# Linear attention with every query normalized, then three more blocks: norms by quarters of tokens, and an earlier start of factors and projections

## The chip, the cores and the metric

The kernel runs on one core of a Trainium2 chip. A core has a matrix engine (TensorE, here PE, with its weight loads as PEld), a vector engine (VectorE, DVE), an activation engine (ScalarE, ACT), a general engine (GpSimd, POOL) and queues that move data (issued by SyncE, SP). Each engine takes its instructions in order, and they wait for one another by semaphores. Matrix results land in eight banks of PSUM, each 128 rows by 512 floats. The metric is the device time of one execution in microseconds (us), lower being better.

## The reference

Four blocks follow one another, each added to its input and normalized over the 256 features: a linear attention, a selected low-rank update, a softmax attention and a mixture of experts. The change touches only the first:

```
q = hidden_states @ Wq.T + bq            # 4 x 512 tokens x 256 -> 16 heads of 128
k, v = ...                               # 4 key heads of 128, each used by 4 query heads
sq, sk = elu(q) + 1, elu(k) + 1
kv = einsum('bhsd,bhse->bhde', sk, v)
norm = einsum('bhsd,bhd->bhs', sq, sk.sum(axis=2))
attn = einsum('bhsd,bhde->bhse', sq, kv) / (norm[..., None] + 1e-6)
x = layernorm(x + attn.reshape(b, s, H * D) @ Wo.T)
```

## The kernel before

`layer0_attention` computes this block, phase 1, one batch of 512 tokens after another; the four batches run the same code. Everything is kept with features on the 128 partitions and the 512 tokens along the row. A product that needs more than one pass of the reduced float type is made from high and low parts of both operands, three matmuls for one (`split_passes`).

For a batch PE does, in this order:

- keys and values for four tiles of 128 tokens (`key_value`), then the sums over tokens (`state`);
- sixteen queries (`query`), one head each, six matmuls of 512 columns into one of three banks `bank_q`. ScalarE makes two passes over it (`query_exp`, lines 426 and 428), VectorE the third (line 522), which gives `sq` and frees the bank;
- between them the eight output maps (`output_map`, line 331): a head pair's kv times Wo, in `bank_a`. ScalarE and VectorE split each into high and low parts (`map_hi`, `map_lo`), of which four pairs are kept;
- four norms (`norm`, line 316), one for every four queries: the sum of sq times the keys' sum for each token. The weights `ksel` are 128x32, so four heads' matmuls stand on four column groups of the array. Norms 0 and 1 make the first half of `bank_n`'s use, norms 2 and 3 the second;
- after norms 1 and 3, VectorE adds a small number and inverts (`invert`, `invert_tokens`), ScalarE and VectorE split the result (`factor_hi`, `parts`) into `rn_parts`;
- sixteen factors (`factor`, line 345): one matmul spreads a head's inverted norm over all partitions, again into one of the three `bank_q`. VectorE multiplies `sq` by it (line 601, signal `scaled`), ScalarE takes the high part `s_hi` (line 468), and the low part `s_lo` is made by VectorE for even n (line 533) and by GpSimd for odd n (line 229);
- sixteen projections (`project`, line 361), twelve matmuls of 256 columns each, from `s_hi`, `s_lo` and a map's parts, all summed in `bank_y`.

The order on each engine is written out by hand. In the last stage PE takes factor n+2, then projection n, with a map behind n = 1, 3, 5 and 7. VectorE scales query n, and for odd n it then makes the low part of n-1:

```python
for n in range(H0):
    dve.wait_ge(bc_done, H0 * b + n + 1)
    dve.tensor_tensor(sq[:, n, :], sq[:, n, :], bank_q[(H0 + n) % 3][:, :], ALU.mult).then_inc(scaled, 1)
    if n % 2 == 1:
        scaled_lo(b, n - 1)
```

`s_hi` and `s_lo` have two buffers, so ScalarE makes the high part of n only when projection n-2 is done. In the texts below, query, factor and projection are counted from 0 to 15, norm from 0 to 3, map from 0 to 7.

Of the kernel before, what the change touches and what calls it, by code (L numbers as in the profile page):

```python
# [10 lines left out]
F32 = mybir.dt.float32  # L11
F32R = mybir.dt.float32r
# [4 lines left out]
P = 128  # L17
# [9 lines left out]
ORDER0 = [(g, j) for j in range(J0) for g in range(G0)]  # L27

# [85 lines left out]
def layer0_attention(nc, a, kept):  # L114

    with ExitStack() as ctx:
# [18 lines left out]
        pick_raw, pick = sb("pick_raw", [H0]), sb("pick", [H0], F32R)  # L135
# [7 lines left out]
        ksel = sb("ksel", [G0, J0, 32])  # L143
# [3 lines left out]
        den, rn = sb("den", [T]), sb("rn", [T])  # L147
        rn_c, rn_parts = sb("rn_c", [T], F32R), sb("rn_parts", [2, T], F32R)
        m_hi, m_lo = sb("m_hi", [4, 2 * D], F32R), sb("m_lo", [4, 2 * D], F32R)
        s_hi, s_lo = sb("s_hi", [2, T], F32R), sb("s_lo", [2, T], F32R)  # L150
# [31 lines left out]
        PARTS_AT = 10  # L182
        MAP_AT = (4, 6, 14, 15)
# [10 lines left out]
        def _(sp):  # L194
# [12 lines left out]
            with sp.Fori(0, B - 1) as b:  # L207
                after = sp.snap(b + 1)
                sp.wait_ge(xT_hi_ready, after)
                sp.wait_ge(xT_lo_ready, after)  # L210
                sp.dma_start(xT[:, :, :], a["xT"][:, bass.ds(after, 1)].rearrange("p o k n -> p (o k) n")).then_inc(xT_in, 16)
# [9 lines left out]
        def _(pool):  # L221
# [3 lines left out]
            def scaled_lo(b, n):  # L225
# [3 lines left out]
                pool.tensor_tensor(s_lo[:, 1, :], sq[:, n, :], s_hi[:, 1, :].bitcast(F32), ALU.subtract).then_inc(s_lo_ready[1], 1)  # L229
# [31 lines left out]
        def _(pe):  # L261
# [30 lines left out]

            def query(b, n):
                g, j = ORDER0[n]
                hd = slice((J0 * g + j) * DH0, (J0 * g + j + 1) * DH0)
                if n < 3:
                    at_least(pe, scaled, H0 * b)
                else:
                    pe.wait_ge(sq_ready, H0 * b + n - 2)
                i = 0  # L300
                for k in range(KD):
                    for lhs, rhs in split_passes(wq_hi[:, k, hd], wq_lo[:, k, hd], xT_hi[:, k, :], xT_lo[:, k, :]):
                        mm = pe.matmul(bank_q[n % 3][:, :], lhs, rhs, start=i == 0, stop=i == 3 * KD - 1)  # L303
# [3 lines left out]
            def norm(b, j):  # L307
# [27 lines left out]
            def factor(b, n):  # L335
# [5 lines left out]
                if n < 3:  # L341
                    pe.wait_ge(sq_ready, H0 * b + H0 + n - 2)
                else:
                    pe.wait_ge(scaled, H0 * b + n - 2)
                pe.matmul(bank_q[(H0 + n) % 3][:, :], pick[:, h:h + 1].broadcast_to([P, P]), rn_parts[:, n // (H0 // 2), :],  # L345
                          start=True, stop=True).then_inc(bc_done, 1)

            def project(b, n):
# [8 lines left out]
                for t in range(NT):  # L357
                    tok = slice(t * P, (t + 1) * P)
                    for i, (lhs, rhs) in enumerate(split_passes(s_hi[:, n % 2, tok], s_lo[:, n % 2, tok], m_hi[:, m, cols], m_lo[:, m, cols])):
# [9 lines left out]
            def body(b, first):  # L369
                pe.wait_ge(xT_hi_ready, b + 1)  # L370
                pe.wait_ge(xT_lo_ready, b + 1)
# [11 lines left out]
                for n in range(3, H0):  # L383
# [3 lines left out]
                    if n % G0 == 1 and n > G0:  # L387
                        norm(b, n // G0 - 1)
# [16 lines left out]
        def _(act):  # L405
            def split_x(b):
                act.wait_ge(xT_in, 16 * (b + 1))
                at_least(act, q_done, H0 * b)
                act.activation(xT_hi[:, :, :], xT[:, :, :], ACT.Copy).then_inc(xT_hi_ready, 1)
# [6 lines left out]
            def factor_hi(b, half_):  # L416
                act.wait_ge(rn_ready, 2 * (2 * b + half_ + 1))
# [3 lines left out]
            def query_exp(b, n):  # L421
# [4 lines left out]
                act.activation(eq[:, n % 3, :], bank_q[n % 3][:, :], ACT.Relu, bias=bq_neg[:, h:h + 1], scale=-1.0).then_inc(eq_capped, 1)  # L426
# [1428 lines left out]
```

## Time and profile before

| | us |
|---|---|
| Runs, median of 3 (lowest to highest) | 835.08 (834.54 to 848.41) |
| The profiled execution | 842.74 |
| its span, first to last instruction | 840.7 |
| PE busy, weight loads beside it | 723.7, 486.0 |
| DVE busy | 528.6 |
| ACT busy | 410.0 |
| POOL busy | 106.4 |

The profile comes from one execution. Busy time is the time in which an engine had an instruction under way. Matmuls are pipelined: one begins before the one ahead has ended, so a matmul's own length is more than the pace at which they follow one another, and the pace is read from the starts. A line of the timeline gives the start, the length, the engine, the line of the code, what is written from what, and in brackets the idle time ahead and who ended it.

### The profile page before, as it was taken

To read this page: it belongs to the slowest core of one execution; us is meant where nothing else is said; L and a number is where in the kernel's file an instruction comes from. 1 tells how busy PE (TensorE), PEld (TensorE's weight loads), DVE (VectorE), ACT (ScalarE), POOL (GpSimd) and SP (SyncE) were. 2 spreads that over 40 slices of the span, in tenths; PEclk is the share of its full clock that TensorE was granted. 3 is DMA by queue.
4 is the path that set the end of the run, shared out by engine and by line. 5 is a ranking of instruction groups with operands and counts; after the bars stand their busy time and mean duration, and the time that the engine had idled before them with its cause. 6 is when DMAs were issued, how large, how long until landed. Compare 5 with 4: busy or idle time off the path is not lost.

```text
span 840.7 us, 10896 instructions
## 1 busy us (share of the span) xinstructions
PE 723.7 (86%) x3836; PEld 486.0 (58%) x3836; DVE 528.6 (63%) x1135; ACT 410.0 (49%) x742; POOL 106.4 (13%) x102
## 2 busy tenths in 40 slices
PE   4798999889989998934678998899999999999764
PEld 3667886778768776833433453355555545455454
DVE  3568556855586558553365777777978787762243
ACT  3474347434754465421202674576556665556422
POOL 0301320132013301315000100010002000000000
PEclk9999999999999999975755896899999999879968
DMA  9200000010000100010650182028100840000000
GB/s 350 76 1 0 27 0 1 1 40 0 0 0 0 69 0 0 0 47 1 75 75 2 23 102 29 2 38 95 23 2 17 93 70 2 1 2 27 26 0 26
DMA packets 13588, 28.22 MB, mean 34 GB/s; under 512 B 2593, under 2 KB 3433, under 8 KB 13033
## 3 DMA queue, kind: packets, MB, share of 16 engines
q1 hardware_dynamic: 13544, 27.67, 17.6%
q8 instruction: 24, 0.39, 0.2%
q14 instruction: 20, 0.16, 0.1%
HBM read 12.59 MB, written 2.10 MB: 17 GB/s over the span
## 4 chain that ended last, share of the span: by engine, by line
PE 39%; DVE 10%; ACT 3%; issue 2%; DMA 2%; POOL 1%; SPq 0%; ACTq 0%; POOLq 0%; DVEq 0%
PE bank_st L1012 8%; PE bank_c L1025 6%; DVE nmax L1512 5%; PE side L962 4%; PE side L1083 3%; PE bank_s L993 3%; PE side L1114 2%; PE side L1043 2%; PE side L945 1%; DMA ks<-qk_lo 1%; PE side L914 1%; PE side L976 1%; ACT xk L1249 1%; DVE ln_bn L1470 1%; PE bank_t L1033 1%
## 5 line engine op out<-in xcount | busy, mean ns | idle before, releaser
L1512 DVE TENSOR_REDUCE nmax<-bank_s 128x1 f32<-128x512 f32 x256 | 164.8, 685 | 75.6 <-PE bank_s L993 74.8
L1293 ACT ACTIVATE shared<-bank_st 128x512 f32<-128x512 f32 x256 | 139.1, 596 | 78.2 <-PE bank_st L1012 77.4
L993 PE MATMUL bank_s<-ks,qs 48*128 48x512 f32 x256 | 117.6, 526 | 19.4 <-DVE nmax L1512 11.6
L1012 PE MATMUL bank_st<-qs,ks 50*128 50x512 f32 x256 | 106.2, 487 | 8.3 <-ACT shared L1293 4.7
L361 PE MATMUL bank_y<-m_hi,s_lo 128*128 128x256 f32 x256 | 75.4, 294 | 16.4 <-ACT s_hi L468 8.4
L522 DVE SCALAR_TENSOR_TENSOR sq<-bank_q,bq,eq 128x512 f32<-128x512 f32 x64 | 46.6, 738 | 51.3 <-ACT eq L428 51.3
L468 ACT ACTIVATE s_hi<-sq 128x512 fp32r<-128x512 f32 x64 | 40.4, 631 | 78.8 <-PE bank_y L361 66.1
L1025 PE MATMUL bank_c<-shared,v 128*32 128x512 f32 x512 | 76.9, 676 | 0.9 <-ACT shared L1293 0.9
L1012 PEld LDWEIGHTS bank_st<-qs,ks 50*128 50x128 f32 x256 | 43.2, 201 | 57.3 <-issue 32.1
L361 PE MATMUL bank_y<-m_lo,s_hi 128*128 128x256 f32 x256 | 73.9, 288 | 0.0
L361 PE MATMUL bank_y<-m_hi,s_hi 128*128 128x256 f32 x256 | 73.7, 288 | 0.0
L229 POOL TENSOR_TENSOR s_lo<-sq,s_hi 128x512 fp32r<-128x512 f32 x32 | 43.4, 1355 | 225.2 <-ACT s_hi L468 225.2
L993 PEld LDWEIGHTS bank_s<-ks,qs 48*128 48x128 f32 x256 | 47.5, 209 | 38.9 <-DVE nmax L1512 29.7
L601 DVE TENSOR_TENSOR sq<-sq,bank_q 128x512 f32<-128x512 f32 x64 | 43.4, 679 | 32.5 <-PE bank_q L345 32.5
L361 PEld LDWEIGHTS bank_y<-m_hi,s_lo 128*128 128x128 f32 x256 | 50.3, 197 | 21.8 <-issue 13.0
L426 ACT ACTIVATE eq<-bank_q,bq_neg 128x512 f32<-128x512 f32 x64 | 44.1, 689 | 35.1 <-PE bank_q L303 33.4
L303 PE MATMUL bank_q<-xT_hi,wq_lo 128*128 128x512 f32 x128 | 54.7, 427 | 0.0
L361 PEld LDWEIGHTS bank_y<-m_lo,s_hi 128*128 128x128 f32 x256 | 50.4, 197 | 1.7
L303 PE MATMUL bank_q<-xT_lo,wq_hi 128*128 128x512 f32 x128 | 50.6, 396 | 0.0
L303 PE MATMUL bank_q<-xT_hi,wq_hi 128*128 128x512 f32 x128 | 50.6, 395 | 0.0
L846 POOL TENSOR_TENSOR ln_rstd<-ln_var,half 128x4 f32<-128x4 f32 x12 | 12.1, 1012 | 303.7 <-DVE ln_var L111 303.7
L361 PEld LDWEIGHTS bank_y<-m_hi,s_hi 128*128 128x128 f32 x256 | 50.4, 197 | 0.0
(242 smaller groups left out, 1353.2 us busy)
## 6 DMA issues: line engine op xcount, KB each, us to landing
qs<-qk_hi SPq DMA_DIRECT2D x16, 256.0 KB, 5.5
ks<-qk_hi SPq DMA_DIRECT2D x16, 256.0 KB, 10.0
xT<-in_xT SPq DMA_DIRECT2D x4, 512.0 KB, 5.1
sq<-in_wqT SPq DMA_DIRECT2D x2, 1024.0 KB, 9.0
wo<-in_woT SPq DMA_DIRECT2D x1, 2048.0 KB, 12.6
xs<-in_x SPq DMA_DIRECT2D x1, 2048.0 KB, 17.5
qs<-qk_lo SPq DMA_DIRECT2D x8, 256.0 KB, 7.8
ks<-qk_lo SPq DMA_DIRECT2D x8, 256.0 KB, 10.5
```

The source lines that it names most:

```text
L229: pool.tensor_tensor(s_lo[:, 1, :], sq[:, n, :], s_hi[:, 1, :].bitcast(F32), ALU.subtract).then_inc(s_lo_ready[1], 1)
L303: mm = pe.matmul(bank_q[n % 3][:, :], lhs, rhs, start=i == 0, stop=i == 3 * KD - 1)
L361: mm = pe.matmul(bank_y4[:, t, :], lhs, rhs, start=n == 0 and i == 0 and t % 2 == 0, stop=n == H0 - 1 and i == 2, skip_group_check=True)
L426: act.activation(eq[:, n % 3, :], bank_q[n % 3][:, :], ACT.Relu, bias=bq_neg[:, h:h + 1], scale=-1.0).then_inc(eq_capped, 1)
L468: act.activation(s_hi[:, n % 2, :], sq[:, n, :], ACT.Copy).then_inc(s_hi_ready, 1)
L522: dve.scalar_tensor_tensor(out=sq[:, n, :], in0=bank_q[n % 3][:, :], scalar=bq1[:, h:h + 1], in1=eq[:, n % 3, :], op0=ALU.add, op1=ALU.max ...
L601: dve.tensor_tensor(sq[:, n, :], sq[:, n, :], bank_q[(H0 + n) % 3][:, :], ALU.mult).then_inc(scaled, 1)
L993: pe.matmul(bank_s[u % 2][:, :], qs[part, b % 2, slot, t * P:(t + 1) * P], ks[part, b % 2, slot, :], start=True, stop=True).then_inc(s_don ...
L1012: pe.matmul(bank_st[u % 2][:, :], ks[part, b % 2, slot, kt * P:(kt + 1) * P], qs[part, b % 2, slot, :], start=True, stop=True).then_inc(st ...
L1025: mm = pe.matmul(bank_c[32 * j:32 * j + 32, :], v[:, b % 2, kt, 4 * g + j, :], probs[:, (4 * s + j) % SLOTS, :], start=kt == 0, stop=kt == 3)
L1293: act.activation(probs[:, u % SLOTS, :], bank_st[u % 2][:, :], ACT.Exp, scale=SCALE1).then_inc(p_ready, 1)
L1512: dve.tensor_reduce(nmax[:, g, t, j:j + 1], bank_s[u % 2][:, :], AX.X, ALU.max, negate=True).then_inc(max_ready, 1)
```

## The change

The norms are taken by quarters. A norm's four matmuls of 512 columns become sixteen of 128 columns, whose weights put each quarter of the tokens in rows of its own, so that the inverted norms of all 512 tokens fill 128 columns. The additions, inversions and splits on VectorE and ScalarE shrink from 512 columns to 128. A factor's one matmul of 512 columns becomes four of 128, each with another column of `pick` as weights.

The order is rewritten. Factors 0, 1 and 2 and projections 0 and 1 stand between queries 12 and 15, and the three banks are taken in turn by queries and factors together (`USES`). From projection 3 on, PE takes factor n+1 and then projection n. The maps are made after queries 4, 6, 8 and 10 and projections 3, 5, 7 and 9. `s_hi` and `s_lo` get three buffers. The splits of x and the statistics are cut in parts.

```diff
+USES = ([("query", n) for n in range(13)] + [("factor", 0), ("query", 13), ("factor", 1), ("query", 14), ("factor", 2), ("query", 15)]
+        + [("factor", n) for n in range(3, H0)])
...
-        s_hi, s_lo = sb("s_hi", [2, T], F32R), sb("s_lo", [2, T], F32R)
+        s_hi, s_lo = sb("s_hi", [3, T], F32R), sb("s_lo", [3, T], F32R)
...
-                for g in range(G0):
-                    mm = pe.matmul(bank_n[32 * g:32 * g + 32, :], ksel[:, g, j, :], sq[:, G0 * j + g, :],
-                                   start=j % 2 == 0, stop=j % 2 == 1)
+                for q in range(QUARTERS):
+                    tok = slice(q * P, (q + 1) * P)
+                    for g in range(G0):
+                        mm = pe.matmul(bank_n[32 * g:32 * g + 32, (j // 2) * P:(j // 2 + 1) * P], ksel[:, g, QUARTERS * (j % 2) + q, :],
+                                       sq[:, G0 * j + g, tok], start=j % 2 == 0 and q == 0, stop=j % 2 == 1 and q == QUARTERS - 1)
...
-                pe.matmul(bank_q[(H0 + n) % 3][:, :], pick[:, h:h + 1].broadcast_to([P, P]), rn_parts[:, n // (H0 // 2), :],
-                          start=True, stop=True).then_inc(bc_done, 1)
+                q_bank_free(b, "factor", n)
+                for q in range(QUARTERS):
+                    mm = pe.matmul(q_bank("factor", n)[:, q * P:(q + 1) * P], pick[:, QUARTERS * h + q:QUARTERS * h + q + 1].broadcast_to([P, P]),
+                                   rn_parts[:, n // (H0 // 2), :], start=True, stop=True)
+                mm.then_inc(bc_done, 1)
...
                 pe.wait_ge(setup_done, 4)
                 factor(b, 0)
+                query(b, 13)
+                norm(b, 2)
                 factor(b, 1)
-                norm(b, J0 - 1)
-                for n in range(H0):
-                    if n + 2 < H0:
-                        factor(b, n + 2)
+                query(b, 14)
+                project(b, 0)
+                factor(b, 2)
+                query(b, 15)
+                project(b, 1)
+                factor(b, 3)
+                project(b, 2)
+                norm(b, 3)
+                for n in range(3, H0):
+                    if n + 1 < H0:
+                        factor(b, n + 1)
                     project(b, n)
-                    if n % 2 == 1 and n < 8:
-                        output_map(b, 4 + n // 2)
+                    if n in (3, 5, 7, 9):
+                        output_map(b, 4 + (n - 3) // 2)
...
-                    act.wait_ge(scaled, H0 * b + n + 1)
-                    at_least(act, y_done, H0 * b + max(0, n - 1))
-                    act.activation(s_hi[:, n % 2, :], sq[:, n, :], ACT.Copy).then_inc(s_hi_ready, 1)
+            def scaled_hi(b, n):
+                act.wait_ge(scaled, H0 * b + n + 1)
+                at_least(act, y_done, H0 * b + max(0, n - 2))
+                act.activation(s_hi[:, n % 3, :], sq[:, n, :], ACT.Copy).then_inc(s_hi_ready, 1)
...
+                scale(b, 0)
+                query(b, 12)
+                scaled_lo(b, 0)
+                scale(b, 1)
+                query(b, 13)
+                query(b, 14)
+                scale(b, 2)
+                scaled_lo(b, 2)
+                query(b, 15)
+                scale(b, 3)
+                scale(b, 4)
+                invert(b, 1)
+                scaled_lo(b, 4)
+                for n in range(5, H0):
+                    scale(b, n)
+                    if n % 2 == 1 and n > 5:
                         scaled_lo(b, n - 1)
```

What stands in PE's row, first batch, at the turn from queries to projections. L303 is a query, L345 a factor, L316 a norm, L361 a projection. Before, from the end of query 15:

```order
L303 MATMUL bank_q<-xT_hi,wq_hi 128x512
L331 MATMUL bank_a<-wo,kvT 128x256 [waits m_lo_ready]
L331 MATMUL bank_a<-wo,kvT 128x256
L345 MATMUL bank_q<-rn_parts,pick 128x512 [waits sq_ready,parts_ready,setup_done]
L345 MATMUL bank_q<-rn_parts,pick 128x512 [waits sq_ready]
L316 MATMUL bank_n<-sq,ksel 32x512 [waits sq_ready]
L316 MATMUL bank_n<-sq,ksel 32x512 x3
L345 MATMUL bank_q<-rn_parts,pick 128x512 [waits sq_ready]
L361 MATMUL bank_y<-m_hi,s_lo 128x256 [waits m_lo_ready,s_lo_ready_even,s_hi_ready]
```

After the change, from factor 1 on; L361 is now the factor, L319 a query, L334 the norm and L378 the projection:

```order
L361 MATMUL bank_q<-rn_parts,pick 128x128 [waits sq_ready]
L361 MATMUL bank_q<-rn_parts,pick 128x128 x3
L319 MATMUL bank_q<-xT_hi,wq_lo 128x512 [waits scaled]
...
L378 MATMUL bank_y<-m_hi,s_lo 128x256 [waits m_lo_ready,s_lo_ready_even,s_hi_ready]
...
L361 MATMUL bank_q<-rn_parts,pick 128x128 [waits sq_ready]
L361 MATMUL bank_q<-rn_parts,pick 128x128 x3
L319 MATMUL bank_q<-xT_hi,wq_lo 128x512 [waits scaled]
...
L378 MATMUL bank_y<-m_hi,s_lo 128x256 [waits s_lo_ready_odd,s_hi_ready]
```

Before, three factors and the last norm stood between the last query and the first projection. After it, projection 0 follows query 14 and projection 1 follows query 15, and each has one factor fewer ahead of it.

VectorE's row in the last stage, after the change, from the scaling of query 7. L571 scales, L565 makes the low part of an even query, L559 that of a map, L518 that of x:

```order
L571 TENSOR_TENSOR sq<-sq,bank_q 128x512 [waits sq_ready,bc_done]
L565 TENSOR_TENSOR s_lo<-sq,s_hi 128x512 [waits scaled,s_hi_ready]
L571 TENSOR_TENSOR sq<-sq,bank_q 128x512 [waits sq_ready,bc_done]
L559 TENSOR_TENSOR m_lo<-bank_a,m_hi 128x512 [waits m_hi_ready]
L571 TENSOR_TENSOR sq<-sq,bank_q 128x512 [waits sq_ready,bc_done]
L565 TENSOR_TENSOR s_lo<-sq,s_hi 128x512 [waits scaled,s_hi_ready]
L518 TENSOR_TENSOR xT_lo<-xT,xT_hi 128x512 [waits q_done,xT_hi_ready]
```

These are the scaling of 7, the low part of 6, the scaling of 8, a map, the scaling of 9, the low part of 8: as before the change, the low part of an even query stands behind the scaling of the next query. What moved is PE's side, where the factor of that next query has one projection less of lead.

## Rows read from the trace of the kernel before

**Rows 1.** Windows: us, busy time and count by engine, granted clock, DMA share, GB/s
```profile
51.80:104.40 52.60, 47.81 (x299) 39.85 (x298) 36.62 (x48) 26.47 (x42) 10.32 (x8) 0.97 0.03 11
136.16:190.67 54.51, 48.05 (x299) 39.87 (x298) 37.93 (x57) 26.46 (x42) 11.36 (x8) 0.97 0.06 16
222.41:276.45 54.04, 47.84 (x299) 39.72 (x298) 37.93 (x57) 26.46 (x42) 11.37 (x8) 0.97 0.00 0
308.20:360.50 52.30, 46.64 (x299) 38.43 (x297) 36.35 (x56) 25.41 (x41) 10.31 (x8) 1.00 0.00 0
360.50:840.70 480.20, 403.71 (x2014) 223.90 (x2012) 307.97 (x794) 229.38 (x463) 39.00 (x50) 0.84 0.25 34
```

**Rows 2.** Timeline of PE, second batch, a norm and an output map among queries
```profile
137.33 0.39 PE L303 MATMUL bank_q<-xT_hi,wq_hi 128*128 128x512 f32 x1
...
138.99 0.39 PE L303 MATMUL bank_q<-xT_lo,wq_hi 128*128 128x512 f32 x1
...
147.54 0.39 PE L303 MATMUL bank_q<-xT_lo,wq_hi 128*128 128x512 f32 x1
147.77 0.39 PE L303 MATMUL bank_q<-xT_hi,wq_hi 128*128 128x512 f32 x1
...
149.10 0.40 PE L303 MATMUL bank_q<-xT_lo,wq_hi 128*128 128x512 f32 x1
```

**Rows 3.** Timeline of PE, the same batch, factors two projections and a map apart
```profile
161.28 0.58 PE L345 MATMUL bank_q<-rn_parts,pick 128*128 128x512 f32 x1
...
165.47 0.58 PE L345 MATMUL bank_q<-rn_parts,pick 128*128 128x512 f32 x1
```

**Rows 4.** Waits of PE from 30 to 361: us in total, times, longest
```profile
PE bank_n L316 <- DVE sq L522: 6.7, 8, 1.1
```

**Rows 5.** Timeline of PE, second batch: first projection, and the batch's end
```profile
155.93 0.36 PE L361 MATMUL bank_y<-m_hi,s_lo 128*128 128x256 f32 x1 [1.78 <-ACT s_hi L468]
...
180.88 0.36 PE L361 MATMUL bank_y<-m_hi,s_lo 128*128 128x256 f32 x1 [1.46 <-POOL s_lo L229]
...
182.38 0.40 PE L345 MATMUL bank_q<-rn_parts,pick 128*128 128x512 f32 x1
...
189.16 0.36 PE L361 MATMUL bank_y<-m_hi,s_lo 128*128 128x256 f32 x1 [0.87 <-POOL s_lo L229]
```

**Rows 6.** Windows: a stretch just behind the turn of the second batch
```profile
156.30:159.60 3.30, 3.30 (x17) 3.20 (x17) 3.30 (x4) 0.63 (x1) 0.79 (x1) 0.51 0.02 5
```

**Rows 7.** Groups by form, second to fourth batch: busy, mean ns of one
```profile
L522 DVE SCALAR_TENSOR_TENSOR sq<-bank_q,bq,eq 128x512 f32<-128x512 f32 x48 | 34.9, 738 | 33.8 <-ACT eq L428 33.8
...
L544 DVE RECIPROCAL rn<-den 128x256 f32<-128x256 f32 x12 | 20.9, 1746 | 0.1
...
L426 ACT ACTIVATE eq<-bank_q,bq_neg 128x512 f32<-128x512 f32 x48 | 33.1, 689 | 20.7 <-PE bank_q L303 19.4
```

**Rows 8.** Timeline of PE and of its loads (PEld), same batch
```profile
123.95 0.95 PE L290 MATMUL bank_a<-ones,sk_sum 128*128 128x1 f32 x8
...
152.65 0.16 PEld L316 LDWEIGHTS bank_n<-sq,ksel 128*32 128x32 f32 x8 [1.12 <-DVE sq L522]
...
180.85 0.19 PEld L361 LDWEIGHTS bank_y<-m_hi,s_lo 128*128 128x128 f32 x1 [1.75 <-ACT s_hi L468]
180.96 0.19 PEld L361 LDWEIGHTS bank_y<-m_lo,s_hi 128*128 128x128 f32 x1
```

**Rows 9.** Timelines of DVE, ACT and POOL, the end of the same batch
```profile
182.81 0.69 DVE L601 TENSOR_TENSOR sq<-sq,bank_q 128x512 f32<-128x512 f32 x1 [1.53 <-PE bank_q L345]
184.46 0.69 DVE L601 TENSOR_TENSOR sq<-sq,bank_q 128x512 f32<-128x512 f32 x1 [0.96 <-PE bank_q L345]
185.07 0.68 DVE L533 TENSOR_TENSOR s_lo<-sq,s_hi 128x512 fp32r<-128x512 f32 x1
...
186.95 0.63 ACT L468 ACTIVATE s_hi<-sq 128x512 fp32r<-128x512 f32 x1 [2.03 <-PE bank_y L361]
...
187.74 1.28 POOL L229 TENSOR_TENSOR s_lo<-sq,s_hi 128x512 fp32r<-128x512 f32 x1 [2.69 <-ACT s_hi L468]
```

More of the change, by code:

```diff
@@ L291, in state, with q_bank_free @@
                 mm.then_inc(ksum_done, 1)
+            def q_bank_free(b, kind, n):
+                k = USE[kind, n]
+                if k < 3:
+                    at_least(pe, scaled, H0 * b)
+                elif USES[k - 3][0] == "query":
+                    pe.wait_ge(sq_ready, H0 * b + USES[k - 3][1] + 1)
+                else:
+                    pe.wait_ge(scaled, H0 * b + USES[k - 3][1] + 1)
             def query(b, n):
@@ L295, in query @@
                 hd = slice((J0 * g + j) * DH0, (J0 * g + j + 1) * DH0)
[L296 to L299, printed above, removed]
+                q_bank_free(b, "query", n)
                 i = 0
@@ L302, in query @@
                     for lhs, rhs in split_passes(wq_hi[:, k, hd], wq_lo[:, k, hd], xT_hi[:, k, :], xT_lo[:, k, :]):
-                        mm = pe.matmul(bank_q[n % 3][:, :], lhs, rhs, start=i == 0, stop=i == 3 * KD - 1)
+                        mm = pe.matmul(q_bank("query", n)[:, :], lhs, rhs, start=i == 0, stop=i == 3 * KD - 1)
                         i += 1
@@ L382, in body @@
                 pe.wait_ge(wo_in, 16)
-                for n in range(3, H0):
+                for n in range(3, 13):
                     query(b, n)
@@ L521, in query @@
                 dve.wait_ge(eq_ready, H0 * b + n + 1)
-                dve.scalar_tensor_tensor(out=sq[:, n, :], in0=bank_q[n % 3][:, :], scalar=bq1[:, h:h + 1], in1=eq[:, n % 3, :],
+                dve.scalar_tensor_tensor(out=sq[:, n, :], in0=q_bank("query", n)[:, :], scalar=bq1[:, h:h + 1], in1=eq[:, n % 3, :],
                                          op0=ALU.add, op1=ALU.max).then_inc(sq_ready, 1)
@@ L584, in body @@
                     for r in range(2):
-                        cp = dve.tensor_copy(dst[:, 4 * r:4 * r + 3 * 33 + 1:33], bank_a[1][:, g:g + 1].broadcast_to([P, J0]))
+                        cp = dve.tensor_copy(dst[:, 16 * r:16 * r + 7 * 33 + 1:33], bank_a[1][:, g:g + 1].broadcast_to([P, 2 * QUARTERS]))
                 cp.then_inc(ksel_ready, 1)
-                for n in range(3, H0):
+                for n in range(3, 12):
                     query(b, n)
+                    if n in (3, 5) and last:
+                        residual_stats(b - 1, (0, 1) if n == 3 else (2, 3))
                     if n == 7 and last:
-                        residual_stats(b - 1)
-                    if n == PARTS_AT:
+                        residual_merge(b - 1)
+                    if n == 9:
                         invert(b, 0)
-                    if n in (PARTS_AT, PARTS_AT + 1):
-                        invert_tokens(b, 0, n - PARTS_AT)
-                    if n == PARTS_AT + 4:
+                    if n == 10:
                         parts(b, 0)
@@ L622, in _ @@
             residual(B - 1)
-            residual_stats(B - 1)
+            residual_stats(B - 1, range(NT))
+            residual_merge(B - 1)
 def by_tile(x):
@@ L1795, in constants @@
         for j in range(J0):
-            pick[32 * g + j, J0 * g + j] = pick[32 * g + 4 + j, J0 * g + j] = 1.0
-            part_c[32 * g + j], part_c[32 * g + 4 + j], part_m[32 * g + 4 + j] = 1.0, -1.0, 1.0
+            for q in range(QUARTERS):
+                row, col = 32 * g + QUARTERS * (j % 2) + q, QUARTERS * (J0 * g + j) + q
+                pick[row, col] = pick[row + 16, col] = 1.0
+                part_c[row], part_c[row + 16], part_m[row + 16] = 1.0, -1.0, 1.0
     return {"pick": pick, "part_c": part_c, "part_m": part_m, "ones": np.ones((P, 1), np.float32),
```

108 lines of the change are left out of this document (54 added, 54 removed).

## The prediction

> **What bounds the kernel now.** I first cut the span into stretches [rows 1]. The attention phase takes 360.5 us and the rest 480.2 us; the diff touches only the first. The first four rows are the piece of each batch that the change rebuilds, from query 9 (the tenth) to the end of projection 15: 52.60, 54.51, 54.04 and 52.30 us, mean 53.36. In each of them PE is busy for some 48 us and no other engine for more than 38, so PE is what there is to shorten, by taking away work or waits.
>
> The PE timeline of the second batch gives the prices of its work. A query matmul follows the one before after 0.23 us, so a query (six) is 1.40 [rows 2]. A norm: from 137.33 to 138.99 is 1.66 us, less two of these paces, 1.19. An output map: 147.77 to 149.10 is 1.33, less the same, 0.86 [rows 2]. Between the factors at 161.28 and 165.47 lie two projections, two factors and a map: 4.19 us without a gap [rows 3]. A factor is one 512-column matmul of the query's pace, 0.235, so a projection is (4.19 - 0.86 - 0.47)/2 = 1.43. The sum from query 9 on: 7 queries 9.8, 3 norms 3.6, 16 factors 3.8, 16 projections 22.9, 6 maps 5.2, together 45.2 us. What is left, 53.36 - 45.2 = 8.2 us a batch, is waiting and slow clock, and that is all a new order can win.
>
> Where it sits: PE waits for the last query of norm 2 and again for that of norm 3, 6.7 us in eight waits, 0.84 each [rows 4]. For the first scaled query it waits 1.78, and near the end for GpSimd's low part, 1.46 and 0.87 us [rows 5]. After the gaps of the turn from queries to projections the granted clock is 0.51 for 3.3 us, the 1.2 GHz level [rows 6]; that costs about 1.6. It happens in three of the four batches.
>
> **The change part by part.** *The turn.* Factors 0 to 3 and projections 0 to 2 move between the queries. They give PE work where it waited for norm 3 and for the first scaled query. I replayed the new order by hand with the prices above (and those of factor and norm below), from query 9 at 0: norm 1 at 1.40, query 10 at 2.74, the map 4.14, query 11 at 5.00, query 12 at 6.40, factor 0 from 7.80 to 8.24. Query 13 takes the bank of query 11, since a factor now has a turn in the three banks, so it waits until VectorE has finished query 11. That is some 0.2 for the last matmul's way out (0.39 long at a pace of 0.23 [rows 2]), 0.69 on ScalarE [rows 7] and again 0.63, as its pass for a high part [rows 9], 0.74 on VectorE [rows 7] and some 0.07 between: 8.73, and 8.78 with a guess of 0.05 until PE starts, a wait of 0.55. From there norm 2 runs at 10.2, factor 1 at 11.5, query 14 at 12.0, projection 0 at 13.4, factor 2, query 15 to 16.6, projection 1, factor 3, projection 2 to 19.9. ScalarE has query 15 late, at 18.3, VectorE at 19.1, still ahead of norm 3. Projection 3 begins at 21.8. So of the waits and the slow clock of the turn, some 5 us with 1.6 of clock, nearly all is won.
>
> *Smaller factors on VectorE.* The reciprocals go from four of 128x256, 1.75 us each [rows 7], to two of 128x128 a batch, at half the elements for half the price, so 5.2 us of VectorE. It was not the bound; worth nothing but the earlier factors, which are in the replay. Halved splits of x, split statistics and the third buffer are hidden likewise: the third buffer takes away the waits of the batch's end, since a high part no longer waits for the projection just before. Without this cover they cost 1.46 and 0.87 again.
>
> *A factor in four matmuls.* Each quarter has its own weights (another column of pick), so each needs a 128x128 load. The trace has no matmul of 128 columns in the reduced float type. From below: columns alone, a quarter of 0.235 each, so 0 more per factor. From above: eight one-column matmuls with 128x128 loads take 0.95 us, 0.12 each [rows 8]. After a gap the next load starts 0.11 after the first [rows 8], and a queued load has nothing else to wait for there. I take 0.11 a quarter, 0.44 a factor, nearer the upper row: +0.2 x 16 = +3.3 us a batch. The Trainium skill, "TensorE: Matmul & The Clock Gate", LDWEIGHTS, says the load takes its columns over 1.2 GHz, 107 ns; the spacing agrees. The same page, Back-to-back issue gap, gives about 81 ns a matmul for a stream of loads and 128-column matmuls; by that a factor would be 0.32 and the batch 1.9 us shorter than I say.
>
> *A norm in sixteen matmuls.* The columns are as many as before, in rounds of four on four column groups. From below nothing more; from above each of eight rounds shows its load, about 0.11, so +0.85. The eight loads of a norm all pass in 0.16 us from its start, while its first matmuls stream [rows 8]: the second set is loaded behind the first. So I stay low: +0.15 a norm, 0.6 a batch. The same page, Part 3, says that a load overlaps matmuls in flight only when their row groups differ; here they are the same. That speaks against this change and is rival C.
>
> *The lead of the factors.* This is the term I rest on. Before, PE issued factor n+2 ahead of projection n; now factor n+1. VectorE still makes the low part of an even query n only after it has scaled query n+1. So an even projection waits for a chain that starts with the factor just ahead of it. Its price: factor to scaling 0.43 (182.38 to 182.81) [rows 5, 9], of which 0.235 is the factor's own; in quarters the last starts at 0.33 and its columns and way out take 0.25, so 0.58. Then scaling holds VectorE 0.60, and the low part takes 0.68 [rows 9]; 0.05 until PE starts, the guess above. Sum 1.91 us from the factor's start, while PE has 0.44 to do: it waits 1.47. That is so for n = 6, 8, 10, 12, 14: 7.35 a batch. Nothing is queued that could fill it, as PE goes in order; factor n+2, behind it, is late by as much, so the wait comes back at each even projection. An odd projection's chain: 0.58, scaling 0.69, ScalarE 0.63, GpSimd 1.28, with 0.04, 0.16 and 0.14 between [rows 9], 3.5 us from its factor. For n = 7 to 13 PE reaches it at 1.91 + 1.43 + 0.44 = 3.8, no wait. For n = 5, whose even neighbour has no such wait, 1.1; 0.2 each at n = 3 and 15.
>
> **The sum.** Waits after: 0.55 + 0.2 + 1.1 + 7.35 + 0.2 = 9.4. Work: 45.2 + 3.3 + 0.6 = 49.1. A batch has 58.5 us against 53.36, +5.1; four of them +20. The profiled execution was 842.74 us (span 840.7) and would be 863; the median is 835.08, 7.7 lower, and the same step on it gives 855. The spread of the runs shown, 834.54 to 848.41, is likely the clock of the later phase (0.84 granted [rows 1]), which I hold equal.
>
> **The rivals.** A, as above: 855. Its own range is 849 to 862: a norm's extra between 0 and 0.3 instead of 0.15 is 2.4 either way, and the later phase may move by a few us.
> B, a quarter costs its columns only (0.06): a batch is 16 x 0.2 = 3.2 us shorter, four 12 to 13: 843. For it: loads run beside matmuls in all of [rows 3]; against: the 0.11 spacing of [rows 8].
> C, the small tiles' loads show: 0.7 us more in each of 16 norms, +11: 866. Against it the eight loads in 0.16 us.
> D, the waits pull the clock down again: three gaps in a row of 1.47 us. Each stretch like [rows 6] costs 1.6; with two or three a batch, +16: 871. Against it: gaps of 1.46 to 0.87 us a few us apart at the end of a batch [rows 5] went with no fall.
> E, no waits at the even projections, the other side. The place is the head of projections 6 to 14. If the third buffer and one factor of lead were enough, the 7.35 us go: 855 - 29 = 826. It decides where such a wait is under (7.35 - 5.1)/5 = 0.45 us instead of 1.47; at 0.45 the time is that of before. For it: in [rows 3] the chain never shows. Against: there the factor led by two projections, and the order rows put scaling n+1 ahead of low part n.
>
> **How the numbers follow.** Chances: A 0.50, B 0.17, C 0.10, D 0.09, E 0.14. The likeliest is A, 855. The range of 838 to 868 leaves out E and most of D, and holds B and C. A measurement here can tell about 2% from no change: below 818.4 or above 851.8. Slower: C, D and 0.38 out of A, 0.57. Within: B, 0.10 out of E and 0.12 out of A, 0.39. Faster: what is left of E, helped by the later phase's clock, 0.04.
>
> **What would show it.** PE gaps of about 1.5 us ahead of projections 6, 8, 10, 12 and 14, released by VectorE's low part; none at 7 to 13 odd; a pair of projections every 6.1 us with a map, 5.2 without, where it is 4.19 now. Loads of the quarters 0.11 apart. A norm of 1.2 to 1.4 us. Granted clock 1.00 from query 9 to the end of each batch. The span after the attention phase within a few us of 480. I am wrong if the even gaps are under 0.5 us (E), if the quarters are 0.06 apart (B), or if the later phase moves by more than 10 us.

## The result, and the profile after

| | before | after |
|---|---|---|
| Runs beside each other, median (lowest to highest) | 840.54 (834.54 to 848.41), 4 | 863.66 (859.31 to 868.02), 4 |
| The profiled execution | 842.74 | 859.31 |
| its span | 840.7 | 857.5 |

The change makes the kernel slower: the ratio of the times is 1.03, with a 95% interval of 1.0168 to 1.0431. The four runs of after lie in two pairs, near 859.5 and 867.8; the profile is of one of the lower pair.

The windows of after, cut as [rows 1] cut before. The columns are us, busy time and count of PE, PEld, DVE, ACT and POOL, granted clock, DMA share, GB/s:

```profile
52.64:110.61 57.97, 49.34 (x416) 44.70 (x415) 29.19 (x47) 24.52 (x42) 10.92 (x8) 1.00 0.03 10
143.25:201.45 58.20, 49.48 (x416) 44.74 (x415) 29.69 (x52) 24.52 (x42) 10.79 (x8) 1.00 0.06 15
234.09:292.27 58.18, 49.47 (x415) 44.70 (x414) 29.69 (x52) 24.52 (x42) 10.80 (x8) 1.00 0.00 0
324.91:383.00 58.09, 49.38 (x415) 44.63 (x413) 28.54 (x50) 23.49 (x40) 10.31 (x8) 1.00 0.00 0
383.00:857.50 474.50, 396.64 (x2014) 220.62 (x2013) 308.67 (x794) 228.89 (x463) 38.91 (x50) 0.85 0.25 34
```

The attention phase ends at 383.0 instead of 360.5, +22.5 us. The phase behind it, whose code is the same, took 474.5 instead of 480.2, 5.7 less at a clock of 0.85 instead of 0.84. Together that is the +16.8 of the two spans. From query 9 to projection 15 a batch takes 58.11 in the mean. In after the third map stands ahead of query 9 (behind query 8), so the same work as in [rows 1] is that plus a map of 0.86: 58.97 against 53.36, +5.6 a batch, +22.4 in four. The clock is 1.00 in each of the four; before it was 0.97 in three of them.

PE's waits in the attention phase (us in total, times, longest):

```profile
PE bank_y L378 <- ACT s_hi L459: 20.0, 14, 1.4
PE bank_y L378 <- DVE s_lo L565: 8.3, 6, 1.4
...
PE bank_y L378 <- POOL s_lo L238: 4.3, 4, 1.1
PE bank_q L319 <- DVE sq L554: 1.8, 4, 0.4
```

L378 is the projection, L319 a query. Of before, the waits for norms of [rows 4], 6.7 us, are gone, and so are those for the first scaled query. In their place stand twenty waits of 1.4 us, 28.3 us in two rows, five in each batch.

One of them, the timeline of PE in the first batch around projection 8 (start, length, engine, line, operation, and in brackets the idle time ahead and who is held to have ended it):

```profile
84.40 0.36 PE L378 MATMUL bank_y<-m_hi,s_lo 128*128 128x256 f32 x1 [1.43 <-ACT s_hi L459]
...
88.47 0.74 PE L361 MATMUL bank_q<-rn_parts,pick 128*128 128x128 f32 x4
90.64 0.35 PE L378 MATMUL bank_y<-m_hi,s_lo 128*128 128x256 f32 x1 [1.43 <-ACT s_hi L459]
...
92.14 0.56 PE L361 MATMUL bank_q<-rn_parts,pick 128*128 128x128 f32 x4
92.54 0.33 PE L378 MATMUL bank_y<-m_hi,s_lo 128*128 128x256 f32 x1
92.71 0.28 PE L378 MATMUL bank_y<-m_lo,s_hi 128*128 128x256 f32 x1
...
96.88 0.35 PE L378 MATMUL bank_y<-m_hi,s_lo 128*128 128x256 f32 x1 [1.43 <-ACT s_hi L459]
...
102.25 0.36 PE L378 MATMUL bank_y<-m_hi,s_lo 128*128 128x256 f32 x1 [1.43 <-ACT s_hi L459]
```

and what the other engines do in it, over the gap from 89.2 to 90.64:

```profile
89.25 0.69 DVE L571 TENSOR_TENSOR sq<-sq,bank_q 128x512 f32<-128x512 f32 x1 [1.46 <-PE bank_q L361]
89.85 0.69 DVE L565 TENSOR_TENSOR s_lo<-sq,s_hi 128x512 fp32r<-128x512 f32 x1
89.97 0.63 ACT L459 ACTIVATE s_hi<-sq 128x512 fp32r<-128x512 f32 x1 [1.60 <-DVE sq L571]
```

At 88.47 PE issues factor 9. VectorE sat idle until it came (1.46), scales query 9 at 89.25, and only then makes the low part of query 8, from 89.85 to 90.54. PE starts projection 8 at 90.64. The row names ScalarE, but that instruction is the high part of query 9, which projection 8 does not use and which ended at 90.60 by chance; the other six of the twenty waits do name VectorE's low part. At 92.54 projection 9 follows its factor without a wait.

### The profile page after: what moved, and what is told of

It reads as the page before. It is cut to its first block, busy times and chain, and to the rows that moved or that the text cites. A ratio compares the mean times of both kernels' runs of the same rounds, so it can differ in the third digit from the quotient of the medians.

```text
span 857.5 us, 12122 instructions
## 1 busy us (share of the span) xinstructions
PE 727.3 (85%) x4412; PEld 508.7 (59%) x4412; DVE 504.4 (59%) x1131; ACT 405.2 (47%) x746; POOL 106.1 (12%) x102
## 4 chain that ended last, share of the span: by engine, by line
PE 36%; DVE 10%; ACT 3%; issue 2%; DMA 2%; POOL 1%; SPq 0%; ACTq 0%; POOLq 0%; DVEq 0%
PE bank_st L1059 8%; PE bank_c L1072 6%; DVE nmax L1559 5%; PE side L1130 3%; PE side L1009 3%; PE bank_s L1040 2%; PE side L1161 2%; DMA ks<-qk_lo 1%; PE side L992 1%; PE side L1090 1%; PE side L961 1%; ACT xk L1296 1%; DVE ln_bn L1517 1%; PE side L1023 1%; PE bank_t L1114 1%
## 5 line engine op out<-in xcount | busy, mean ns | idle before, releaser
L1059 PE MATMUL bank_st<-qs,ks 50*128 50x512 f32 x256 | 104.3, 479 | 9.2 <-ACT shared L1340 5.7
L378 PE MATMUL bank_y<-m_hi,s_lo 128*128 128x256 f32 x256 | 76.1, 297 | 33.0 <-ACT s_hi L459 20.0
L571 DVE TENSOR_TENSOR sq<-sq,bank_q 128x512 f32<-128x512 f32 x64 | 43.9, 686 | 81.5 <-PE bank_q L361 81.5
L1072 PE MATMUL bank_c<-shared,v 128*32 128x512 f32 x512 | 73.8, 650 | 0.9 <-ACT shared L1340 0.9
L378 PE MATMUL bank_y<-m_lo,s_hi 128*128 128x256 f32 x256 | 72.2, 282 | 0.0
L378 PE MATMUL bank_y<-m_hi,s_hi 128*128 128x256 f32 x256 | 72.1, 282 | 0.0
L378 PEld LDWEIGHTS bank_y<-m_hi,s_lo 128*128 128x128 f32 x256 | 48.6, 190 | 37.0 <-ACT s_hi L459 21.6
L452 ACT ACTIVATE eq<-bank_q,bq_neg 128x512 f32<-128x512 f32 x64 | 43.9, 686 | 35.7 <-PE bank_q L319 33.8
L319 PE MATMUL bank_q<-xT_hi,wq_lo 128*128 128x512 f32 x128 | 54.9, 429 | 1.8 <-DVE sq L554 1.8
L319 PE MATMUL bank_q<-xT_lo,wq_hi 128*128 128x512 f32 x128 | 50.5, 395 | 0.0
L319 PE MATMUL bank_q<-xT_hi,wq_hi 128*128 128x512 f32 x128 | 50.5, 394 | 0.0
L378 PEld LDWEIGHTS bank_y<-m_lo,s_hi 128*128 128x128 f32 x256 | 48.8, 191 | 0.4
L378 PEld LDWEIGHTS bank_y<-m_hi,s_hi 128*128 128x128 f32 x256 | 48.7, 190 | 0.0
```

The lines of the kernel that those rows point to most:

```text
L319: mm = pe.matmul(q_bank("query", n)[:, :], lhs, rhs, start=i == 0, stop=i == 3 * KD - 1)
L378: mm = pe.matmul(bank_y4[:, t, :], lhs, rhs, start=n == 0 and i == 0 and t % 2 == 0, stop=n == H0 - 1 and i == 2, skip_group_check=True)
L452: act.activation(eq[:, n % 3, :], q_bank("query", n)[:, :], ACT.Relu, bias=bq_neg[:, h:h + 1], scale=-1.0).then_inc(eq_capped, 1)
L571: dve.tensor_tensor(sq[:, n, :], sq[:, n, :], q_bank("factor", n)[:, :], ALU.mult).then_inc(scaled, 1)
L1059: pe.matmul(bank_st[u % 2][:, :], ks[part, b % 2, slot, kt * P:(kt + 1) * P], qs[part, b % 2, slot, :], start=True, stop=True).then_inc(st ...
L1072: mm = pe.matmul(bank_c[32 * j:32 * j + 32, :], v[:, b % 2, kt, 4 * g + j, :], probs[:, (4 * s + j) % SLOTS, :], start=kt == 0, stop=kt == 3)
```

## Experiments

All compute the whole result. The end of the attention phase is the start of its last residual addition: 360.74 in before, 383.27 in after. "Period" is the time from one batch's first key matmul to the next one's: 86.26 and 85.78 in before, 90.84 and 90.82 in after.

**1. The lead of the factors, alone.** After with one factor more of lead from projection 3 on, nothing else:

```diff
                 norm(b, 3)
+                factor(b, 4)
                 for n in range(3, H0):
-                    if n + 1 < H0:
-                        factor(b, n + 1)
+                    if n + 2 < H0:
+                        factor(b, n + 2)
                     project(b, n)
```

> The changed kernel with one edit: in the last stage PE issues factor n+2 ahead of projection n, as before the change (factor 4 stands ahead of the loop). Theory of the lead: a factor now starts 2.3 us or more ahead of the even projection that waits for its chain of 1.9 us, so the five waits of 1.43 us a batch and the 1.1 us at projection 5 go. A pair of projections with a map comes every 4.6 us instead of 6.24. The period of a batch falls from 90.8 us by 8, the time by some 32, to 828 to 833, below the kernel before. Rival, the array or ScalarE is the bound anyway (the profile names ScalarE's high part as the releaser of most of these waits): the waits stay at 1 us or more, the time stays above 850.

Measured: 829.25 (828.49 to 830.49), before beside it 842.7, ratio 0.9868 (0.9793 to 0.9944). The attention phase ends at 347.59. The same view of waits as above:

```profile
PE bank_q L319 <- DVE sq L555: 1.8, 4, 0.4
...
PE bank_y L378 <- POOL s_lo L238: 0.9, 4, 0.3
```

All twenty waits are gone. The pair of projections with a map, from factor to factor on PE's timeline:

```profile
168.38 0.74 PE L361 MATMUL bank_q<-rn_parts,pick 128*128 128x128 f32 x4
168.96 0.33 PE L378 MATMUL bank_y<-m_hi,s_lo 128*128 128x256 f32 x1
...
173.00 0.74 PE L361 MATMUL bank_q<-rn_parts,pick 128*128 128x128 f32 x4
```

4.62 us, where after has 6.24 (84.40 to 90.64). The edit issues each factor one projection earlier and gives back 34.4 us of the median and 35.7 of the attention phase; so the missing lead is the cause, and the rest of the change is worth a gain. A batch's period falls by 9.1 (90.84 to 81.75).

**2. The same waits, from VectorE's side.** After with the low part of an even query put ahead of the scaling of the next one:

```diff
                 for n in range(5, H0):
                     scale(b, n)
-                    if n % 2 == 1 and n > 5:
-                        scaled_lo(b, n - 1)
...
+                    if n % 2 == 0:
+                        scaled_lo(b, n)
```

> The changed kernel with one edit: PE keeps its lead of one, but VectorE makes the low part of an even query right after its own scaling and its map, ahead of the scaling of the next query. Theory of the lead: even projections no longer wait for the next factor; now each projection waits for its own factor's chain, 2.7 us for even and 3.5 for odd against 2.3 of PE work ahead. Waits of about 0.4 at even and near 1 at odd projections, a pair with a map every 5.8 us instead of 6.24, 5.0 instead of 5.37 without. Some 8 us less, 850 to 855. Rival, that the order on VectorE has no part in it: the waits stay at the even projections with 1.4 us each, and the time stays at 860.

Measured: 853.62 (852.04 to 860.1), ratio 1.0183 (1.0094 to 1.0271). This is within the expected range and 10.0 less than after. PE's timeline, second batch, every wait from 176.5 on:

```profile
180.82 0.36 PE L378 MATMUL bank_y<-m_hi,s_lo 128*128 128x256 f32 x1 [1.09 <-POOL s_lo L238]
186.72 0.36 PE L378 MATMUL bank_y<-m_hi,s_lo 128*128 128x256 f32 x1 [1.09 <-POOL s_lo L238]
192.09 0.36 PE L378 MATMUL bank_y<-m_hi,s_lo 128*128 128x256 f32 x1 [1.42 <-ACT s_hi L459]
197.11 0.36 PE L378 MATMUL bank_y<-m_hi,s_lo 128*128 128x256 f32 x1 [1.47 <-POOL s_lo L238]
```

The even projections no longer wait at all, not even the 0.4 us that I had expected. But now the odd ones wait for GpSimd's low part, whose chain is longer: 1.09 in the pairs with a map, which come every 5.90 (180.82 to 186.72) instead of 6.24, and 1.42 and 1.47 in those without (the first of them is put down to ScalarE again). So the order on VectorE decides which projection waits. It also decides a part of what is lost, 10.0 us of the 34.4 that the lead gives back; but with one factor of lead there is a wait in every pair.

**3. The quarters, alone.** Norms and factors in quarters, in the order, the lead and the two buffers of before:

```diff
+USES = [("query", n) for n in range(H0)] + [("factor", n) for n in range(H0)]
...
                 factor(b, 1)
...
+                norm(b, J0 - 1)
+                for n in range(H0):
+                    if n + 2 < H0:
+                        factor(b, n + 2)
+                    project(b, n)
+                    if n % 2 == 1 and n < 8:
+                        output_map(b, 4 + n // 2)
```

> The kernel before with the quarters alone: norms in sixteen matmuls, factors in four, inversions of 128 columns; the order on every engine, the lead of two and the two buffers are those of before. Load-bound quarters (0.10 to 0.11 us each): +0.2 us for each of 64 factors, +13, less up to 1 us a batch for VectorE's shorter inversions at the turn: 9 to 13 us more than before. Rival, a quarter costs its columns only: no more than before, or 2 us less.

Measured: 848.13 (845.64 to 853.13), ratio 1.0073 (1.0036 to 1.0111), 5.4 us over before, less than expected. The profiled execution was the longest of the eleven, 853.13, and its attention phase ends at 368.75, 8.0 later than before's. The waits:

```profile
PE bank_y L377 <- ACT s_hi L449: 8.5, 4, 2.2
...
PE bank_y L377 <- POOL s_lo L237: 3.1, 4, 0.9
PE bank_n L333 <- DVE sq L543: 2.1, 4, 0.5
```

Before has 8.4, 7.6 and 6.7 in the rows that answer. What I had left out is that longer factors also fill gaps: the factors' extra work is 16 x 0.2 x 4 = 13, and in these rows the waits fell by 9.0, from 22.7 to 13.7. The sum, some 4, is in line with the median; the profiled execution has some 4 more. These are in the granted clock. The first projection now waits 2.15 where it waited 1.78 [rows 5], and behind it the clock falls, as in [rows 6]. Its timeline and its window:

```profile
157.88 0.55 PE L377 MATMUL bank_y<-m_hi,s_lo 128*128 128x256 f32 x1 [2.15 <-ACT s_hi L449]
```

```profile
157.80:162.00 4.20, 4.12 (x19) 4.16 (x20) 0.85 (x2) 0.63 (x1) 1.25 (x1) 0.50 0.00 0
```

It falls in all four batches, and for longer in two of them. The windows of the second and the fourth batch:

```profile
136.00:194.60 58.60, 54.80 (x431) 49.63 (x430) 33.78 (x58) 27.85 (x46) 10.32 (x8) 0.94 0.06 15
309.00:368.75 59.75, 55.98 (x436) 50.69 (x434) 31.73 (x57) 27.76 (x45) 10.31 (x8) 0.94 0.00 0
```

The first and the third have 0.97, and [rows 1] has 0.97 three times and 1.00 once. The missing share of each window, times its length, is an estimate of what the slow clock cost: some 10.5 us here and 4.8 in before, 5 to 6 more, which covers those 4.

**4. The order, alone.** The order, lead and three buffers of after, with whole norms and factors; only what whole tiles need is moved (inversions in two pieces, the split one query later):

```diff
-                for q in range(QUARTERS):
-                    mm = pe.matmul(q_bank("factor", n)[:, q * P:(q + 1) * P], pick[:, QUARTERS * h + q:QUARTERS * h + q + 1].broadcast_to([P, P]),
-                                   rn_parts[:, n // (H0 // 2), :], start=True, stop=True)
+                mm = pe.matmul(q_bank("factor", n)[:, :], pick[:, h:h + 1].broadcast_to([P, P]), rn_parts[:, n // (H0 // 2), :],
+                               start=True, stop=True)
...
                     if n == 9:
                         invert(b, 0)
+                        invert_tokens(b, 0, 0)
                     if n == 10:
+                        invert_tokens(b, 0, 1)
+                    if n == 11:
                         parts(b, 0)
...
                 invert(b, 1)
                 scaled_lo(b, 4)
+                invert_tokens(b, 1, 0)
```

> The new order alone: norms, factors and inversions whole as before the change, order, lead of one and three buffers as after it (the two halves of an inversion and the split stand one query later where they must). Theory of the lead: the waits at even projections stay, 1.5 us each; a pair with a map comes every 5.85 us instead of 6.24, since a factor is 0.2 shorter and the chain 0.15; the first factor waits up to 2 us for the longer inversion. In sum 3 to 9 us less than the changed kernel, and 10 to 16 more than before. Rival, the quarters are what makes the change slow: about the time of before or less.

Measured: 865.93 (864.46 to 866.91), ratio 1.0307 (1.0229 to 1.0386). The pair is as expected, 5.85 (PE's timeline, second batch, projections 6 and 8):

```profile
178.49 0.36 PE L375 MATMUL bank_y<-m_hi,s_lo 128*128 128x256 f32 x1 [1.43 <-ACT s_hi L456]
...
184.34 0.36 PE L375 MATMUL bank_y<-m_hi,s_lo 128*128 128x256 f32 x1 [1.43 <-ACT s_hi L456]
```

The waits of 1.43 stay with whole factors, so the quarters don't make them. But the time is 2.3 us more than that of after, where I had expected 3 to 9 less. Each batch loses elsewhere, on the same timeline at factor 0 and in the window behind it:

```profile
153.94 0.50 PE L358 MATMUL bank_q<-rn_parts,pick 128*128 128x512 f32 x1 [2.52 <-DVE rn_parts L584]
```

```profile
153.90:158.00 4.10, 4.05 (x15) 2.11 (x15) 2.04 (x3) 1.60 (x4) 0.00 (x0) 0.58 0.00 0
```

The longer inversions and splits come 2.5 us too late for factor 0, and the clock falls behind that gap in three of the four batches. In the first it does not:

```profile
63.00:67.10 4.10, 3.94 (x20) 2.36 (x21) 2.72 (x6) 2.16 (x4) 0.00 (x0) 1.00 0.01 4
```

Further on, a reciprocal of the second inversion stands in VectorE's row ahead of the scaling of query 5, and projection 5 waits 1.39 where it waits 1.09 in after. Projection 3 waits 0.74 too, which these rows don't place. In all, GpSimd's low parts are waited for in 8.4 us of this kernel and in 4.3 of after. So the quarters do buy something: the early start of the factors.

**5. The third buffer.** Experiment 1 with two buffers, and before with three:

```diff
-                at_least(act, y_done, H0 * b + max(0, n - 2))
-                act.activation(s_hi[:, n % 3, :], sq[:, n, :], ACT.Copy).then_inc(s_hi_ready, 1)
+                at_least(act, y_done, H0 * b + max(0, n - 1))
+                act.activation(s_hi[:, n % 2, :], sq[:, n, :], ACT.Copy).then_inc(s_hi_ready, 1)
```

> The kernel with factors leading by two, with two buffers of scaled queries instead of three. If the third buffer is what takes away the waits of the batch's end: a high part waits for the projection two ahead, then 0.8 us to its end and 1.6 for GpSimd's low part, 2.4 against 1.9 of PE work where no map lies between, so waits of 0.5 us at projections 13 and 15, smaller ones elsewhere; 1 to 2 us a batch, 833 to 837 against 829. Rival, with the lead of two the buffers are never waited for: 829 as with three.

Measured: 835.42 (826.22 to 836.6), before beside it 842.4, ratio 0.9897 (0.9859 to 0.9936). The batch's end on PE's timeline:

```profile
180.15 0.36 PE L378 MATMUL bank_y<-m_hi,s_lo 128*128 128x256 f32 x1 [0.38 <-ACT s_hi L460]
...
184.13 0.36 PE L378 MATMUL bank_y<-m_hi,s_lo 128*128 128x256 f32 x1 [0.87 <-POOL s_lo L238]
```

These are projections 13 and 15. The last is the 0.87 of [rows 5] again. In the same batch of before projection 11 waits 1.46 and projection 13 waits 0.77; here nothing is left of the first and 0.38 of the second. What made the 1.46 is in before's timelines of GpSimd and VectorE: the low part of query 11 and the split of x in the second batch, and the same low part in the fourth, which has no split behind it:

```profile
178.39 1.22 DVE L486 TENSOR_TENSOR xT_lo<-xT,xT_hi 128x1024 fp32r<-128x1024 f32 x1
178.40 2.34 POOL L229 TENSOR_TENSOR s_lo<-sq,s_hi 128x512 fp32r<-128x512 f32 x1 [2.90 <-ACT s_hi L468]
...
349.58 1.28 POOL L229 TENSOR_TENSOR s_lo<-sq,s_hi 128x512 fp32r<-128x512 f32 x1 [2.89 <-ACT s_hi L468]
```

Started just behind the split, the low part took 2.34 us instead of 1.28, and projection 11 waits 1.46 instead of 0.41. Where the low part starts first, it keeps its length, and the split is the longer one. So it is in before's first batch (1.29 and 2.29) and in experiment 3:

```profile
183.34 1.29 POOL L237 TENSOR_TENSOR s_lo<-sq,s_hi 128x512 fp32r<-128x512 f32 x1 [3.32 <-ACT s_hi L449]
183.49 1.68 DVE L507 TENSOR_TENSOR xT_lo<-xT,xT_hi 128x512 fp32r<-128x512 f32 x1
```

So about 1.05 of the 1.46 came from the split beside it. That the longer factors of the quarters, 0.2 each, cover the other 0.4 fits experiment 3, where projection 11 doesn't wait, but no run shows it alone. The other way round, in before:

```diff
-                    at_least(act, y_done, H0 * b + max(0, n - 1))
-                    act.activation(s_hi[:, n % 2, :], sq[:, n, :], ACT.Copy).then_inc(s_hi_ready, 1)
+                    at_least(act, y_done, H0 * b + max(0, n - 2))
+                    act.activation(s_hi[:, n % 3, :], sq[:, n, :], ACT.Copy).then_inc(s_hi_ready, 1)
```

> The kernel before with three buffers of scaled queries and nothing else. The waits for GpSimd's low part (7.6 us in nine) and the short ones for ScalarE's high part behind the first projection (some 1.4 us) go: 7 to 9 us less than before, ratio 0.990. Those at the turn (1.78 us at the first projection, 0.84 at norms 2 and 3) and the slow clock behind it stay. Rival, the low part is late because of VectorE's split of x beside it: the 1.46 us waits stay, and only 3 us go.

Measured: 837.16 (830.5 to 838.34), ratio 0.9945 (0.9903 to 0.9987). The attention phase ends at 352.13, 8.6 earlier, and no wait for GpSimd is left in it. (I had expected 7 to 9 in the median, which fell by 5.2.)

```profile
PE bank_y L361 <- ACT s_hi L468: 7.6, 6, 1.8
PE bank_n L316 <- DVE sq L522: 6.7, 8, 1.1
...
PE bank_y L361 <- DVE s_lo L533: 0.4, 2, 0.2
```

The window of the rest shows where a part of it went in this execution, 483.57 us at 0.83 where [rows 1] has 480.20 at 0.84:

```profile
352.13:835.70 483.57, 408.14 (x2012) 225.48 (x2012) 308.84 (x794) 229.72 (x463) 38.92 (x50) 0.83 0.24 34
```

So the third buffer is worth 8.6 us of the attention phase in the order of before, and 4.0 in that of experiment 1 (351.62 against 347.59), where less was waited for. Some 2 of the 8.6, an estimate from 1.05 in two batches, are the split again: with the third buffer the low part of query 11 starts ahead of it, at 176.65 against 177.40, and takes 1.29.

**6. What the runs point to.** Whole norms and factors (no quarter loads), three buffers, a lead of two, and the turn one query later, so that the longer inversions are in time:

```diff
-                for n in range(3, 13):
+                for n in range(3, 14):
                     query(b, n)
...
+                norm(b, 2)
                 factor(b, 0)
-                query(b, 13)
-                norm(b, 2)
-                factor(b, 1)
                 query(b, 14)
-                project(b, 0)
-                factor(b, 2)
+                factor(b, 1)
                 query(b, 15)
-                project(b, 1)
+                factor(b, 2)
+                project(b, 0)
                 factor(b, 3)
-                project(b, 2)
+                project(b, 1)
                 norm(b, 3)
+                factor(b, 4)
+                project(b, 2)
                 for n in range(3, H0):
-                    if n + 1 < H0:
-                        factor(b, n + 1)
+                    if n + 2 < H0:
+                        factor(b, n + 2)
```

> What the other runs point to: norms, inversions and factors whole as before the change, three buffers, lead of two, and the turn begun one query later so that the longer inversion is done: queries to 13, norm 2, factor 0, query 14, factor 1, query 15, factor 2, projection 0. Against the kernel with the lead of two and quarters each factor is 0.2 us shorter, 3.3 us a batch, less waits of about 0.4 us at factor 0 and 0.7 at projection 1: 2 to 2.5 us a batch less, a period of 79.5 us, 817 to 823. Rival, VectorE with 7 us more of inversions a batch is late at the turn, as in the run with the order alone: 829 or more.

Measured: 824.15 (815.48 to 825.39), ratio 0.9778 (0.9719 to 0.9837). It beats both kernels, before by some 18 us, and lies just above the 817 to 823 expected. The window of one period:

```profile
100.70:180.41 79.71, 77.71 (x458) 63.84 (x457) 53.47 (x88) 42.82 (x69) 15.97 (x12) 1.00 0.04 11
```

79.7 us a period at full clock, 6.3 under before and 2.0 under experiment 1; PE is busy in 77.7 of them. What waits remain in the stage are for the first factors, 0.8 and 0.7 us a batch.

## Why the prediction was right

The likeliest case, A, came out: slower, by the mechanism named, 863.66 where 855 was forecast. The time alone would not have decided it: it lies 1.7 above A's own range (849 to 862) and nearer to rival C's 866. The rows decide for A. By its steps:

- **The lead of the factors.** Forecast: 1.47 ahead of projections 6, 8, 10, 12 and 14. Found: 1.43, or 1.38 where VectorE is named, at these five and at no odd one from 7 to 15. The chain from factor 9 to projection 8 took 2.17; 0.19 of that is the map that is still draining when the factor starts, the rest 1.98 against 1.91. Of the 0.07, 0.05 is PE's start 0.10 after the low part's end instead of my guess of 0.05. Experiments 1 and 2 show the cause from both sides. Rival E, that the wait isn't there, is out.
- **What such a wait costs** is more than its row says. Experiment 1 takes 1.62 from a pair with a map (6.24 to 4.62). The row counts idle time from the end of the last matmul ahead, but the next would have started before that end: 168.38 to 168.96 is 0.58 without the wait, 88.47 to 90.64 is 2.17 with it, 1.59 more. Pairs: 6.1 and 5.2 forecast, 6.24 and, without a map, 5.37 (96.88 to 102.25) found. That is some 0.15 a pair, 0.7 a batch, too little in the sum.
- **Projection 5.** 1.1 forecast; 1.09 in three batches, and in the first:

```profile
80.04 0.36 PE L378 MATMUL bank_y<-m_hi,s_lo 128*128 128x256 f32 x1 [1.01 <-POOL s_lo L238]
```

- **Query 13, projections 3 and 15.** 0.55, 0.2 and 0.2 forecast; query 13 waits 0.44, the other two have no row of their own in the waits above.
- **The turn.** As replayed: PE reaches projection 3 without the waits for norm 3 and for the first scaled query, and the clock stays at 1.00. Rival D (three gaps of 1.4 in a row pull the clock down) is out.
- **A factor in four matmuls.** 0.44 forecast. From 92.14 to 92.54 are 0.40, and the first projection matmul then takes 0.17 until the next one instead of 0.12: 0.45 together. On the timeline of the loads the four lie between 92.03 and 92.48, 0.11 each:

```profile
92.03 0.53 PEld L361 LDWEIGHTS bank_q<-rn_parts,pick 128*128 128x128 f32 x4
92.48 0.19 PEld L378 LDWEIGHTS bank_y<-m_hi,s_lo 128*128 128x128 f32 x1
```

  Rival B (0.24) is out. The Trainium skill, "TensorE: Matmul & The Clock Gate", gives a load its columns over 1.2 in ns, an estimate of 107 ns for 128 (LDWEIGHTS), and a stream of loads and 128-column matmuls about 81 ns a matmul (Back-to-back issue gap); the 0.11 a quarter here agrees with the first.
- **A norm in sixteen matmuls.** +0.15 forecast, none found. In the first batch, on PE's timeline:

```profile
62.89 1.08 PE L334 MATMUL bank_n<-sq,ksel 128*32 128x128 f32 x32
63.90 0.66 PE L361 MATMUL bank_q<-rn_parts,pick 128*128 128x128 f32 x4
```

  and in before, second batch:

```profile
137.65 1.06 PE L316 MATMUL bank_n<-sq,ksel 128*32 128x512 f32 x8
138.65 0.51 PE L303 MATMUL bank_q<-xT_hi,wq_lo 128*128 128x512 f32 x1
```

  1.01 and 1.00 from the norm's start to the next instruction's. The sixteen small loads (with 32 records, where the four had 8) are hidden, and rival C is out. The rule of the Trainium skill, "TensorE: Matmul & The Clock Gate", Part 3, that a load overlaps matmuls in flight only when row groups differ, is not borne out here: these tiles share their rows and differ in columns.
- **The end of the batch.** The prediction laid the 1.46 and 0.87 us of [rows 5] to the buffers, and said that without the third they cost the same again. For the 0.87 experiment 5 bears it out. For the 1.46 it doesn't: about 1.05 of it was VectorE's split of x beside GpSimd, which the change halves and moves, and in experiment 5 nothing of it came back. Both waits are gone in after, as forecast.
- **The sum.** A batch 58.5 forecast, 58.97 found. The 0.7 of the pairs is set off by the norms (0.6) and by waits not seen (some 0.5); some 0.9 a batch, in the starts behind the gaps or elsewhere, isn't placed.
- **The rest of the kernel** I held equal, and it was not: 5.7 us shorter in the profiled execution. In the medians it doesn't show: +23.1 (863.66 less 840.54), against +22.5 of the attention phase and +20 forecast. The median of before in the runs of the result, 840.54, is 5.5 above the 835.08 on which I put the step; that and the 3 us in the step make the 8.7 us between 855 and 863.66. The range, up to 868, held it, and some of that is luck: two of the four runs, 867.64 and 868.02, lie at its very edge, and the 8 us between the pairs are as much as the whole miss.

## What to carry to other kernels

When an engine works in order, count for each result how many units of other work lie between the instruction that starts its chain and the one that uses its end; here the chain is 1.9 to 3.5 us, one projection of cover too few cost 1.6 us in every pair, and moving one issue ahead by one place gave 34 us. Reordering VectorE alone moved the waits from the even to the odd projections and gave 10. A helper instruction can also be late because of its neighbour on another engine: look at its length in a batch where the neighbour is missing. A gain in smaller helper work counts only for what it lets start earlier: quarters made each factor dearer on the bounding engine by 0.2 us, and the same early start was had, one query later, without them.

## What the runs showed of the hardware

- A matmul of 128 columns with its own 128x128 weights follows the last after 0.11 us, about the load's pace and not the 0.06 of its columns. The norm's small loads, 128x32 on four column groups, cost nothing beside matmuls of 128 columns.
- The granted clock stayed at 1.00 through five gaps of 1.4 us a batch, some 4 us of work apart. It fell to 0.50 and 0.58, at or near the 1.2 GHz level, behind single gaps of 2.15 and 2.52; and before had 0.51 behind its turn with 1.78 at its end. A gap of that length does not always bring it down: it stayed at 1.00 behind the 2.49 of experiment 4's first batch and behind the 1.78 of before's fourth.
- GpSimd's low part and VectorE's split of x, both reading two tiles, did not run side by side at full pace: the one that started second took 1.0 to 1.1 us longer (2.34 instead of 1.28 on GpSimd, 2.29 instead of 1.22 on VectorE).
- The releaser that a wait's row names can be an instruction that ended at nearly the same time: fourteen of the twenty waits name ScalarE, whose result was not the one that was late.
- The phase behind, with the same code, ran between 474.5 us at 0.85 and 483.6 at 0.83 in the profiled executions. A saving of 8.6 us ahead of it showed as 5.2 in the medians.
